# A graph network with a token-choosing feed-forward layer: three small tiles built first, tile 0 woven in later, and a new table of due units

## The reference

```python
def _gcn_conv(x, W, b, src, dst, norm, num_nodes):
    h = x @ W
    agg = jax.ops.segment_sum(h[src] * norm[:, None], dst, num_segments=num_nodes)
    return agg + b
# deg counts dst with one loop a node; dinv = rsqrt(deg); norm = dinv[src] * dinv[dst]
h = relu(conv(layernorm(x), W1, b1)); h = relu(conv(h, W2, b2)); x = x + conv(h, W3, b3)
# then a feed-forward layer on chosen tokens of layernorm(x)
weights = x @ wr + br; idx = top_k(weights, s // 2)[: s // 2 - 1]
y = (gelu(x[idx] @ w1 + b1) @ w2 + b2) * weights[idx];  x = x + scatter(y, idx)
```

## Time and profile before

| | |
|---|---|
| time, median of 3 runs | 1931.12 us (1929.98 to 1933.58) |
| profiled execution: time, span | 1930.19 us, 1928.4 us |
| PE, DVE, ACT, POOL busy | 94%, 56%, 28%, 57% |
| mean granted clock of PE | 0.969 |
| first dense unit, last identity (L906) | 201.32 us, 808.8 us |

### The profile page before, as it was taken

How to read it: one execution, slowest core, us unless ns; L and a number is a source line. 1 busy time by engine, 2 the same in 40 slices (tenths; PEclk the granted TensorE clock), 3 DMA queues, 4 the chain that set the end, 5 groups by cost and what they waited for, 6 DMA issues and landing times.

```text
span 1928.4 us, 28276 instructions
## 1 busy us (share of the span) xinstructions
PE 1822.1 (94%) x10122; PEld 1062.6 (55%) x10122; DVE 1072.2 (56%) x2897; ACT 530.6 (28%) x1127; POOL 1100.4 (57%) x1178
## 2 busy tenths in 40 slices
PE   6874989999999999999999999999999999989998
PEld 4753656666565566545555555554444444446755
DVE  7777988788666666542222222223554556876422
ACT  5724234444444455511111111110000000012021
POOL 5401155766666766347777777745777777721401
PEclk9965899999999999999999999999999999999999
DMA  7568245555556566567776777766888988751200
GB/s 270 168 221 281 87 163 187 175 168 191 199 195 208 185 207 213 204 247 245 251 236 232 238 253 237 235 196 245 310 275 296 319 312 284 268 174 72 83 13 23
DMA packets 170448, 403.37 MB, mean 209 GB/s; under 512 B 29419, under 2 KB 122529, under 8 KB 157640
## 3 DMA queue, kind: packets, MB, share of 16 engines
q1 hardware_dynamic: 119720, 263.44, 38.4%
q0 software_dynamic: 50592, 138.13, 22.9%
HBM read 282.57 MB, written 118.89 MB: 208 GB/s over the span
## 4 chain that ended last, share of the span: by engine, by line
PE 83%; DVE 9%; DMA 3%; ACT 2%; issue 2%; POOL 1%; POOLq 0%; DVEq 0%; another core or an unknown queue 0%; ACTq 0%
PE ag L1300 28%; PE pw L1300 20%; PE ag L1309 10%; PE pw L1267 8%; PE pw L1394 3%; PE pw L1326 2%; PE both L1326 2%; PE ag L1407 2%; PE pw L1407 2%; PE ag L1394 1%; PE both L1318 1%; PE ag L1253 1%; ACT space_ring L1642 1%; DVE space_a L910 1%; DVE space_tables L898 1%
## 5 line engine op out<-in xcount | busy, mean ns | idle before, releaser
L1905 POOL DMA_INDIRECT space_rows<-row_dram,src_s x947 | 951.6, 1005 | 372.2 <-issue 200.2
L1300 PE MATMUL ag<-space_a,space_ring 128*128 128x512 f16 x2107 | 621.5, 380 | 3.9 <-DVE space_work L940 3.8
L1267 PE MATMUL pw<-space_tables 128*128 128x147 f16 (+1 forms) x2022 | 324.2, 247 | 51.3 <-DVE space_tables L898 44.9
L1309 PE MATMUL ag<-space_rows,hots 128*128 128x512 f16 x947 | 358.6, 379 | 6.9 <-DVE space_b L940 5.7
L1267 PEld LDWEIGHTS pw<-space_tables 128*128 128x128 f16 x2022 | 220.6, 116 | 227.8 <-DVE space_tables L898 61.5
L1642 ACT ACTIVATE space_ring<-pw 128x784 f16<-128x784 f32 (+1 forms) x257 | 220.4, 858 | 278.2 <-PE pw L1267 272.7
L898 DVE TENSOR_TENSOR space_tables<-iota_two,space_tables 128x588 f16<-128x588 f16 (+1 forms) x506 | 257.6, 509 | 0.0
L1300 PEld LDWEIGHTS ag<-space_a,space_ring 128*128 128x128 f16 x2107 | 198.0, 97 | 102.4 <-DVE space_work L940 4.0
L894 DVE TENSOR_TENSOR space_tables<-iota_many,space_tables 128x512 f16<-128x512 f16 x506 | 212.8, 421 | 27.4 <-PE pw L1267 24.7
L1300 PE MATMUL pw<-space_b,space_ring 128*128 128x512 f16 x735 | 189.3, 379 | 0.0
L1300 PE MATMUL pw<-space_a,space_ring 128*128 128x512 f16 x686 | 167.2, 379 | 0.0
(11 more groups left out here) (421 smaller groups left out, 1956.4 us busy)
## 6 DMA issues: line engine op xcount, KB each, us to landing
space_ring<-adj SPq DMA_DIRECT2D x48, 1568.0 KB, 7.7
adj<-space_ring SPq DMA_DIRECT2D x34, 1568.0 KB, 6.1
space_tables<-adj SPq DMA_DIRECT2D x17, 1568.0 KB, 7.4
extra<-hots SPq DMA_DIRECT2D x3, 6272.0 KB, 22.4
space_work<-extra SPq DMA_DIRECT2D x147, 128.0 KB
space_rows<-row_dram,src_s POOLq DMA_INDIRECT x947, 4.0
space_b<-in_x_turned SPq DMA_DIRECT2D x7, 896.0 KB, 14.2
space_a<-in_x SPq DMA_DIRECT2D x7, 896.0 KB, 5.9
```

What stands on the lines that cost most here:

```text
L1267: pe.matmul(pw[v % 2][:, half, at_c:at_c + n], olo[:, j % RING // 2, :, j % 2 * 2 + i], ohi[:, j % RING // 2, j % 2, 0:n, i], start=s == F ...
L1300: mm = pe.matmul(bank(q), a[:, k, :], hh[l][:, k, :], start=i == 0 and not own, stop=i == TILES - 1)
L1309: pe.matmul(bank(q), hots_area[:, hot_at, :, g - SPOT_GROUPS[SPOT_GROUP_OF[g]][0]], slots[g % GR], start=i == 1, stop=i == n).then_inc(g_u ...
L1905: pool.indirect_dma_start(slots[g % GR], None, row_dram[STEP_LAYER[g]], bass.IndirectOffsetOnAxis(src_s[:, s:s + 1], 0)).then_inc(g_in[g % ...
```

## The change

1. Tiles 29, 30 and 31 (32 steps each) are built first, then 25 and 26, then 27 and 28 with the groups of tile 0 woven between, then 1 to 24, 32 and 33. `SCAN` is 52.
2. The units of layer 0 follow that order; the units of 29 and 30 alternate row by row, and all 98 stand right behind pair 51. `low_first` and `high_first` run for all 49 row tiles in a run after the factors. The spill's unit moves from 87 to 130.
3. `due_units` is a new rule: in proportion to a cost of the pairs, at most the units of tiles built (`most`), at least what a buffer to be reused needs (`least`).
4. All window rows, all step chunks and edge addresses at once at the beginning; iotas and picks by a finer table of runs (14 and 36 instead of 6 and 31); moments of x on ACT for three of seven groups of row tiles and on DVE (`measure_x`) for four.
5. The digits' one-hots in a layout with four steps innermost; a hot tile in one operation instead of two; degree work in pairs 36 to 51.
6. The clears of `extra` for layers 1 and 2 and of `pair_dram` move from the beginning to units 240 to 940. The exception for tile 1's loops on PE (`PE_LOOPS`) goes.

```diff
+FIRST_BUILT = (29, 30, 31)
+BUILD = [(t, g) for t in FIRST_BUILT + (25, 26) for g in range(GROUPS_OF_TILE)]
+BUILD += [(0, 0)] + [(27, g) for g in range(GROUPS_OF_TILE)]
+BUILD += [(0, 1), (0, 2)] + [(28, g) for g in range(GROUPS_OF_TILE)]
+BUILD += [(0, g) for g in range(3, GROUPS_OF_TILE)]
+BUILD += [(t, g) for t in list(range(1, LAST_BUILT + 1)) + [32, 33] for g in range(GROUPS_OF_TILE)]
...
-FIRST_CHUNKS = 3
+FIRST_CHUNKS = 6
...
-SPILL_AT = [END[0] + 38, START[TILES] + 85, START[2 * TILES] + 85]
-OVER_AT = [SPILL_AT[0] + 45, SPILL_AT[1] + 50, SPILL_AT[2] + 50]
+SPILL_AT = [2 * TILES + 32, START[TILES] + 85, START[2 * TILES] + 85]
+OVER_AT = [SPILL_AT[0] + 2, SPILL_AT[1] + 50, SPILL_AT[2] + 50]
...
 def due_units():
-    due = []
-    ends = [units_until(n) for n in range(TD)]
+    ends = [END[q] for q in DENSE_Q if q < TILES]
+    first = 2 * TILES
+    last = ends[-2] + int(0.3 * (ends[-1] - ends[-2]))
+    cost = [0.0]
     for j in range(NPAIR):
-        total = 0
-        for n in range(1, TD):
-            a, b = TILE_PAIR[n] + SKEW, TILE_PAIR[n + 1] + SKEW
-            done = min(max(j + 1 - a, 0), b - a) / (b - a)
-            total += int(done * (ends[n] - ends[n - 1]))
-        due.append(total)
+        cost.append(cost[-1] + 400 + TILES * WIDTH[WINDOW_OF[min(2 * j, DSTEPS - 1)]])
+    due = [0] * SCAN
+    for j in range(SCAN, NPAIR):
+        want = first + int((last - first) * (cost[j] - cost[SCAN]) / (cost[NPAIR - 1] - cost[SCAN]))
+        most = max([e for e, p in zip(ends, END_PAIR) if p + SKEW <= j + 1])
+        least = first
...
+        due.append(max(due[-1], least, min(most, want)))
     return due
...
-                if j >= LOW_AT:
-                    n = -(-TILES // (SCAN - LOW_AT))
-                    for t in range((j - LOW_AT) * n, min((j - LOW_AT + 1) * n, TILES)):
-                        low_first(t)
+            for t in range(TILES):
+                low_first(t)
...
+            for n in range(len(FIRST_BUILT)):
+                store_tile(n)
```

More of the change, by code:

```diff
@@ L83, in runs_of, with base_runs @@
     return out
-BASE_RUNS = runs_of(0, TD, lambda t: WIDTH_OF[t + 1] == WIDTH_OF[t])
+def base_runs():
+    out, a = [], 0
+    while a < SPARSE0:
+        b = a + 1
+        while b < SPARSE0 and RUN_OF[b] == RUN_OF[a] and BASE[b] - BASE[b - 1] == RUN_OF[a]:
+            b += 1
+        if out and out[-1][1] == a and RUN_OF[a] == out[-1][2] and (b - a) * out[-1][3] == a - out[-1][0] and \
+                BASE[a] == BASE[out[-1][0]] + P * out[-1][3]:
+            out[-1] = (out[-1][0], b, out[-1][2], out[-1][3] + 1)
+        else:
+            out.append((a, b, RUN_OF[a], 1))
+        a = b
+    return out
+RUN_OF.append(RUN_OF[-1])
+BASE_RUNS = base_runs()
+assert [BASE[a] + P * i + w * k for a, b, w, n in BASE_RUNS for i in range(n) for k in range((b - a) // n)] == BASE[:SPARSE0]
 STEP_RUNS = runs_of(0, WN, lambda w: QUOTA[w + 1] == QUOTA[w] and w + 1 != SPARSE0)
@@ L152, in merged @@
 def merged(layer):
-    first = [DENSE[0] - 1] if layer == 1 else []
-    dense = [(t, i) for t in first + [t for t in range(DENSE[layer]) if t not in first] for i in range(TILES)]
+    if layer == 0:
+        tiles = [t for t in BUILT if t < DENSE[0]]
+        dense = [(t, i) for i in range(TILES) for t in tiles[0:2]] + [(t, i) for t in tiles[2:] for i in range(TILES)]
+    else:
+        first = [LAST_BUILT] if layer == 1 else []
+        dense = [(t, i) for t in first + [t for t in range(DENSE[layer]) if t not in first] for i in range(TILES)]
     sparse = []
@@ L227 @@
 SPARSE_STEP = {q: sum(steps_gathered(Q[p]) for p in SPARSE_Q if p < q) for q in SPARSE_Q}
-TILE_PAIR = [FIRST[TILE_WINDOW[n]] // 2 for n in range(TD)] + [NPAIR]
 SKEW = 4
 LOOP_LAG = 6
[L231 to L239, removed]
+SCAN = 52
@@ L252, in due_units @@
     return due
 DUE = due_units()
[L256 to L266, removed]
+BEFORE = 4
+PRODUCT_AT = [t - BEFORE if t < BEFORE else t - BEFORE + 1 for t in range(TILES)]
@@ L272 @@
[L272 to L275, removed]
+SPILL_FIRST_AT = SPOTS_OF_AT + 1
+DEGREES_AT = SPOTS_OF_AT + 2
+DINV_AT = SCAN - 1
+assert BATCH_AT[-1] < DIGITS_AT and SPARSE_DEG_END <= SPOTS_OF_AT and DEGREES_AT < DINV_AT
+assert END_PAIR[len(FIRST_BUILT) - 1] + 4 == SCAN and LOOP_LAG <= 6
+SETTLED_OF = [max(b + 1 for b, cs in enumerate(BATCHES) if cs[0] < CHD and cs[0] <= min(2 * j + 3, DSTEPS - 1) // P) if j < SCAN else 0
@@ L829, in hot_tiles @@
                     c, t = TILE_SPANS[i]
-                    noted(dve.tensor_scalar(tile_base[:, i:i + 1], step_base[:, c, 0:1], float(W - 1 - P * t), None, ALU.add))
-                dve.wait_ge(c_dve, steps["all"])
-                for i in range(first, last_one):
-                    noted(dve.tensor_scalar(tile_hot[:, i], iota16[:, 0:P + 4], tile_base[:, i:i + 1], None, ALU.is_equal),
-                          f"hot tile {i}")
+                    noted(dve.tensor_scalar(tile_hot[:, i], iota16[:, 0:P + 4], float(P * t - W + 1), step_base[:, c, 0:1],
+                                            ALU.add, ALU.is_equal), f"hot tile {i}")
             def step_masks():
@@ L1468, in _ @@
             pe.matmul(disorder, ones[:], order, start=True, stop=True, skip_group_check=True).then_inc(p_order, 1)
-            for t in range(AHEAD_OF_STEPS):
-                if t == 0:
-                    pe.wait_ge(c_dve, steps["centred"])
+            pe.wait_ge(c_dve, steps["centred"])
+            for t in range(BEFORE):
                 product_first(t)
@@ L1482, in chunk_steps @@
                     mm.then_inc(p_steps, 1)
-            pe.wait_ge(c_dve, steps["low of step zero 0"])
-            for c in range(FIRST_CHUNKS):
+            pe.wait_ge(c_dve, steps["low of step zero"])
+            for c in range(CH):
                 chunk_steps(c)
-            for t in range(AHEAD_OF_STEPS, BEFORE):
-                product_first(t)
             def colsums(name):
@@ L1563, in _ @@
             j = SCAN
+            units(2 * TILES)
             while j < NPAIR:
@@ L1718, in _ @@
                 done_stats += 1
-            for t in range(AHEAD_OF_STEPS, BEFORE):
-                out_first(t)
+                if done_stats % 4 == 0:
+                    out_first(done_stats // 4 - 1)
             settle(0)
@@ L1738, in _ @@
                 if j == COUNTS_AT + 1:
[L1739 removed]
+                    for i in range(len(DVE_GROUPS)):
+                        root_of_measured(i)
+                    act.wait_ge(degs_s, 1)
                     act.wait_ge(c_dve, steps["counts read"])
```

376 lines of the change are left out of this document (214 added, 162 removed).

## The result

The changed kernel took 2121.07 us (median of 4 runs, 2115.08 to 2123.35), the kernel before 1931.36 us beside it: a ratio of 1.0976, 95% interval 1.0951 to 1.1002. It is slower, 8 us above the forecast of 2113 and inside the range.

What follows compares the result with a forecast made beforehand. It took PE to bound tile building before, and DVE's one-hots to bound the new stretches of steps alone. 1930 us + 177 for the due table + 6 for the beginning gave 2113 us, range 2042 to 2190.

Steps and rivals of the forecast that it cites:

- The due table, forecast 177 us: Tile building: units come in 23 bursts, steps alone between; DVE sets 291 us where PE needs 114, loss 177 us.
- the two ends given, 129 and 182: Due table's loss: 129 us if DVE fills the ring every burst, 182 if it is no further ahead than one group.
- the beginning: Prologue, scaling and first units up to unit 147, with steps still to do: +6 us, ends -17 to +13.
- Rival 1, the clock: In the stretches the clock falls, so each burst starts at half speed: 42 us or more, 2165 us; chance 0.27.
- Rivals 2 to 4: 2: DVE uses whole ring, 2065 us, 0.14; 3: stretches cost nothing, 1913, 0.05; 4: table binds less, about 1930, 0.04.
- Factors at 160, within 152 to 167: End of the prologue: the reciprocal, at 160.57 before, was taken at T = 160, kept within 152 to 167.
- the delay of the first one-hots: Prologue: all window rows and chunks come first, delaying the first one-hots by some 11 us, bounded by 0 and 20.
- shorter work of DVE as time won up to the factors: Prologue on DVE: fewer one-hot groups 16 us less, digits and hot tiles 5 less, added statistics 17 us more.
- Rows landed at T + 47, unit 147 at T + 82: After the factors at T: scaled rows queue on SP behind tile 31's store, landing T + 47; unit 147 at 242.
- The two waits of 20 us: PE stands still some 20 us at the spill matmul and again at unit 147, for the first sum.
- The rest, forecast 0: Overflow-table clears moved to units 240 to 940 on SP, layers 1 and 2 unchanged: 0, bounded by 5 us.
- What to look for: Profile signs: PE busy 70 to 80% from 250 to 850, some 170 us waiting for one-hots, last identity about 990.

Runs made afterwards that it cites:

- e3: The changed kernel with LAG 7 instead of 5, so DVE does the units' work two pairs later: 2103.91 us (1.0899).
- e4: The changed kernel with a second matmul, times a tile of zeros, behind each step in a stretch without units: 2105.19 us (1.0903).
- e1: The changed kernel with only the due table altered, a finished tile's units spread evenly over the pairs that build the next: 1943.98 us (1.0060).
- e6: The changed kernel with a due table as even as built tiles and the three buffers allow, instead of the spread one: 1934.47 us (1.0016).
- e5: The changed kernel with the spread due table, and the scaled rows' stores put ahead of tile 31's store on SP: 1931.07 us (0.9996).

## Why the prediction was right

*The due table, forecast 177 us.* The runs show the step as it was worked out: DVE sets the stretches (e3, e4), a cycle of 64 steps took 28.7 us, and by the forecast's terms 59 units x 0.243 + 14.75 groups x 0.81 + 1.56 = 27.8; the table as a whole is worth 177 us (e1). The equality is partly luck. The 177 of the forecast were for DVE alone; of the measured 177 some 16 or more are the clock (e4), so DVE's part is about 161. That lies between the two ends given, 129 and 182. The loss also depends on the table that one compares with: e1's leaves DVE as full as PE from 250 to 350, and against the more even one of e6 the table costs 187 us (2121.1 - 1934.5). In the trace the building lost 194 us, 17 more than the forecast gave it, and the beginning -0.3 instead of +6. So the 8 us between forecast and result are in the main what two errors of opposite sign leave.

*Rival 1, the clock.* It was a rival and is part of the truth: behind some stretches the clock falls and behind others not. It was set at 42 to 63 us for a fall in every stretch; 16 are shown.

*Rivals 2 to 4.* They fall. DVE made one group in a burst and not the four of the ring, and a second one changed the time (e3); the limit bound as it was read, and the bursts cost 177 us (e1) and not less than 17.

*Factors at 160, within 152 to 167.* This step failed: the reciprocal came at 171.47 and the first dense unit at 174.64, which the forecast itself had named as a sign of being wrong. The mis-sized term is the delay of the first one-hots, put at 11 us with a bound of 20. They came at 55.6, where the kernel before had its first at 37.5, so the delay was 18:

```profile
L974 DVE TENSOR_TENSOR space_tables<-iota_two,space_tables x506: 451/481/1091, 55.6 to 998.8; 128x588 f16<-128x588 f16 x88, 128x784 f16<-128x784 f16 x81
```

From there on the changed kernel makes up half of it. The one-hots of the digits, on which the degrees wait, began at 117.62, before at 108.35 (the first line is of the kernel before, the second of the kernel after):

```profile
108.35 4.94 DVE L819 TENSOR_TENSOR space_a<-iota,space_rows 128x4592 f16<-128x4592 f16 x1
```

```profile
117.62 3.83 DVE L895 TENSOR_TENSOR space_a<-iota_many,space_rows 128x4608 f16<-128x4608 f16 x2
```

They did become shorter, 3.83 us for both instead of 4.94 and 2.54, but the start was 9 us late and the factors 11. The forecast had counted shorter work of DVE as time won up to the factors; behind the digits it won nothing. From their start to the reciprocal it is 53.85 us, where it was 52.22, although DVE is busy for 16.4 of them and was for 37.3: DVE doesn't set the pace there (window, length, DVE's busy us, granted clock, DMA share, GB/s; the kernel before, then after):

```profile
108.35:160.57 52.22, 37.26 (x154) 0.61 0.49 163
```

```profile
117.62:171.47 53.85, 16.41 (x39) 0.61 0.28 93
```

*Rows landed at T + 47, unit 147 at T + 82.* With T = 171.5, the reciprocal, the rows would be due at 218.5, and they landed at 219.69. That the store of tile 31 holds them up is confirmed by e5, where they landed at 198.38. The two waits of 20 us were 15.51 and 3.87: from landing to the one-hot took 3.3 us (to 222.95) and not 8.3, and from the spill matmul to unit 147 11.8 and not 26.1 (26.1 is counted from ACT's evacuation; from the matmul, at 240.94, it was 26.6). I took both from the kernel before, and there single steps of the same chain were longer. Of the second, the operation of POOL behind the way of the spill's rows to DRAM, with POOL's wait for that way, in the kernel before and then after:

```profile
257.03 5.10 POOL L1897 TENSOR_SCALAR space_rows<-space_rows 128x1 f32<-128x1 f32 x1 [8.68 <-DMA extra<-space_rows]
```

```profile
230.93 0.23 POOL L1955 TENSOR_SCALAR space_rows<-space_rows 128x1 f32<-128x1 f32 x1 [1.78 <-DMA extra<-space_rows]
```

Wait and operation are 13.8 us in one and 2.0 in the other. Why they were longer is not shown; before, DVE ran without a gap beside them, and SP stored tiles. The late T, by 11 us, and the short chain, by 18, cancel in part: unit 147 at 235.7 for 242, and -0.3 us instead of +6 for the beginning.

*The rest, forecast 0.* With the table spread and the queue mended (e5), the remainder of the change is worth -0.2 us (1931.07 against 1931.26, interval 0.9988 to 1.0005). The moved clears, forecast at 0, are within that.

*What to look for.* PE was to be busy for 70 to 80% between 250 and 850, with some 170 us of waits for one-hots. It was 84 to 89% in the hundreds shown above, and the waits listed for that line are 68.6 us. The reason is the busy time of matmuls that stand alone, as said at the page; starts, 0.81 us apart, tell the truth here and busy time does not. The last identity came at 1002.3 for some 990.

## What to carry to other kernels

Where an engine keeps pace only because another one has work beside it, a table of due work has to be even in every stretch of a few pairs, and the sum over the program says nothing: the same units between the same steps cost 177 us here when they came in blocks of some 60. And shorter work on an engine is time won only where that engine sets the pace. A rule of "as asked for, but no more than is ready" makes such blocks as soon as the demand runs ahead of the supply; draw the due numbers before running it. Last, a transfer that waits for something late should not stand on its queue ahead of one that others wait for.

## What the runs showed of the hardware that was not expected

- More matmuls can be faster: with a zero matmul behind each step in the stretches, PE had some 1,400 more, the granted clock stayed at 1.00 in the hundreds shown instead of 0.81 to 0.97, and the time fell by 15.9 us.
- The fall is uneven: with the same stretches of 64 steps, the burst at 570 ran at 1.00 and the one at 597 began at 0.50.
- GpSimd's operations on a small tile took very different times: the addition of 128x256 at the spill took 0.72 us (225.56 above) while DVE stood still, before 2.91 at 242.42 among one-hots that DVE ran without a gap. A busy DVE alone doesn't explain it: there the next addition of that shape took 0.82 us, at 245.51, and the one-hot operation of DVE beside it, at 245.66, 0.98 us, where the next of its kind took 0.45. So now one of the two was longer and now the other; the cause was not tested by itself. The row of the kernel before:

```profile
242.42 2.91 POOL L1892 TENSOR_TENSOR space_rows<-space_rows 128x256 f32<-128x256 f32 x1 [32.96 <-DMA space_rows<-extra,space_rows]
```
